# Attention behind a group norm: ten instead of four value units rounded in two parts, one batch's statistics moved to another engine, and another order at the end

## The reference, cut to what matters

```
h = group_norm(x, 8 groups over channels and positions) * gn_w + gn_b
q = qw h + qb;  k = kw h + kb;  v = vw h + vb            # 1x1 convolutions, C = 128
attn = softmax(q^T k / sqrt(128), over the 1024 keys)    # (4, 1024, 1024)
out  = x + pw (attn v) + pb
```

## Time and profile before

| | us |
|---|---|
| median of three runs | 138.47 |
| the profiled execution, its own time | 138.43 |
| its span | 136.2 |
| PE busy | 127.9 (94% of the span) |
| DVE busy | 101.1 (74%) |
| ACT busy | 70.0 (51%) |
| POOL busy | 40.4 (30%) |

### The profile page before, as it was taken

The page is one execution under the profiler, slowest core; times in us unless marked ns, Lnnn a source line. Parts: engine busy times, 40 slices in busy tenths (PEclk is TensorE's granted clock), DMA queues, the critical chain, the costliest instruction groups (busy, mean ns, idle before and its releaser), DMA issues.

```text
span 136.2 us, 2258 instructions
## 1 busy us (share of the span) xinstructions
PE 127.9 (94%) x759; PEld 111.6 (82%) x759; DVE 101.1 (74%) x172; ACT 70.0 (51%) x118; POOL 40.4 (30%) x39
## 2 busy tenths in 40 slices
PE   5899999949999999999999999999999999999990
PEld 5897878827768888999898898898988999988870
DVE  0577889999998878979689989856977898140222
ACT  4054687755765673547346977474585335331000
POOL 5053005085020251305026695024049220012000
PEclk9999999999999999999999999999999999999999
DMA  4970000001998599889961898899915998989512
GB/s 139 277 278 0 0 5 0 18 23 35 197 212 178 152 216 206 188 218 216 203 188 36 196 212 189 233 204 211 199 70 118 197 212 217 239 184 212 172 39 77
DMA packets 9566, 21.00 MB, mean 154 GB/s; under 512 B 2362, under 2 KB 4052, under 8 KB 9556
## 3 DMA queue, kind: packets, MB, share of 16 engines
q1 hardware_dynamic: 8816, 20.59, 62.1%
q10 hardware_dynamic: 740, 0.28, 0.8%
HBM read 4.07 MB, written 2.11 MB: 45 GB/s over the span
## 4 chain that ended last, share of the span: by engine, by line
PE 65%; SPq 12%; DVE 9%; issue 6%; DMA 5%; DVEq 0%
PE ACC L417 24%; SPq L205 11%; PE S L336 8%; PE S L337 7%; PE S L340 7%; PE A L316 5%; DVE blocks L735 3%; PE S L375 3%; DMA pT<-blocks 2%; DMA x_sb<-x 2%; DVE s_sb L726 2%; PE S L280 2%; PE A L292 1%; DVE bn L651 1%; PE A L293 1%
## 5 line engine op out<-in xcount | busy, mean ns | idle before, releaser
L726 DVE TENSOR_SCALAR_CACHE_REDUCE s_sb<-S,row_term 128x1024 f32<-128x1024 f32 x32 | 40.9, 1279 | 12.1 <-PE S L340 11.9
L417 PE MATMUL ACC<-pT,v 128*128 128x128 f32 (+1 forms) x288 | 45.8, 310 | 0.2 <-DMA pT<-blocks 0.2
L546 ACT ACTIVATE s_sb<-s_sb,rowmin 128x1024 f32<-128x1024 f32 x32 | 36.8, 1151 | 15.5 <-DVE s_sb L726 14.5
L417 PEld LDWEIGHTS ACC<-pT,v 128*128 128x128 f32 x288 | 40.3, 191 | 3.4 <-issue 0.6
L735 DVE STREAM_TRANSPOSE blocks<-s_sb 128x1024 f32<-128x1024 f32 x28 | 34.7, 1239 | 0.0
L336 PE MATMUL S<-h_hi,g_hi 128*128 128x512 f32 x64 | 28.7, 449 | 0.3 <-issue 0.3
L337 PE MATMUL S<-h_lo,g_hi 128*128 128x512 f32 x64 | 25.1, 393 | 0.0
L340 PE MATMUL S<-h_hi,g_lo 128*128 128x512 f32 x64 | 19.9, 392 | 0.0
L887 POOL TENSOR_TENSOR xb<-rden_bc,xb 128x512 f32<-128x512 f32 (+1 forms) x7 | 8.4, 1197 | 24.6 <-DVE rden_bc L755 18.9
L340 PEld LDWEIGHTS S<-h_hi,g_lo 128*128 128x128 f32 x64 | 12.0, 188 | 2.8
L336 PEld LDWEIGHTS S<-h_hi,g_hi 128*128 128x128 f32 x64 | 12.1, 189 | 2.3 <-issue 0.4
(11 more groups left out here) (100 smaller groups left out, 145.7 us busy)
## 6 DMA issues: line engine op xcount, KB each, us to landing
pT<-blocks SPq DMA_DIRECT2D x112, 128.0 KB, 2.5
rden_bc<-row_store SPq DMA_DIRECT2D x6, 256.0 KB, 3.5
x_sb<-x SPq DMA_DIRECT2D x1, 1024.0 KB, 6.6
out<-xb SPq DMA_DIRECT2D x8, 128.0 KB, 2.7
out<-xb SPq DMA_DIRECT2D x4, 256.0 KB, 3.1
x_sb<-x SPq DMA_DIRECT2D x2, 256.0 KB, 3.0
x_sb<-x SPq DMA_DIRECT2D x1, 512.0 KB, 3.9
w_in<-weights ACTq DMA_DIRECT2D x2, 128.0 KB, 3.5
```

The lines of the kernel that those rows point to most:

```text
L417: last = pe.matmul(to, v[:, b % 3, t, :], probs[:, :, t, :], start=(t == 0), stop=(t == KT - 1))
L546: act.activation(s_sb[:, c % 3, :], s_sb[:, c % 3, :], ACT.Exp, bias=rowmin[:, c % CH:c % CH + 1], scale=-1.0, accum_out=den[:, n % 2, k:k ...
L726: dve.tensor_scalar(s_sb[:, c % 3, :], S[:, c % 2, :], row_term[:, b % 2, i:i + 1], None, ALU.add, ALU.min, accum_out=rowmin[:, i:i + 1]). ...
```

## The change

- The split units are now (1,2), (1,3) and all four of sets 3 and 5: ten for four. Quarter u of sets 3 and 5 is rounded in step `FIRST[n] + 7 + u` (17 to 20, and 25 to 28), and its unit is computed in the next step. Set 1's two quarters are rounded at the end of step 10. v is rounded in steps 9, 15 and 23.
- Batch 2's statistics go from DVE to ACT: one pass with a sum (Identity) in step 6, one pass with a sum of squares (Square) in step 7, both writing a full result that nobody reads to the first 1024 columns of `pT`, and three small multiplications. PE takes them in step 8 instead of 7. SP's `move_set(2)` waits for them.
- Batch 1's group statistics go through PE one step earlier (steps 0 and 1), its shift stands ahead of the drain in step 3, and ACT normalises it in steps 3 and 4 instead of 4 and 5. The reciprocals of set 1 are turned in step 10 instead of 9.
- On DVE the row terms stand right behind the drain, ahead of the block transposes.
- At the end chunks 30 and 31 are two products of 128 columns each. Chunk 30's stands where the pair stood, chunk 31's at the very end; each is finished and stored by itself.

```diff
-TURN_STEPS = (3, 9, 11, 15, 19, 23, 27)
+TURN_STEPS = (3, 10, 11, 15, 19, 23, 27)
-DEVIATION_STEPS = (1, 7, 16)
-VARIANCE_STEPS = (2, 8, 17)
-EARLY_STATS_STEPS = (5, 6)
-SPLIT_SETS = (3, 5)
+DEVIATION_STEPS = (0, 8, 16)
+VARIANCE_STEPS = (1, 9, 17)
+CHANNEL_STEPS = (6, 7)
+SPLIT_UNITS = ((1, 2), (1, 3), (3, 0), (3, 1), (3, 2), (3, 3), (5, 0), (5, 1), (5, 2), (5, 3))
+SPLIT_SETS = (1, 3, 5)
+ROUND_V_STEPS = (9, 15, 23)
+    FIRST_QUARTERS = {FIRST[n] + 7: SPLIT_UNITS.index((n, 0)) for n in (3, 5)}
+    SECOND_QUARTERS = {FIRST[n] + 7 + u: SPLIT_UNITS.index((n, u)) for n in (3, 5) for u in (1, 2, 3)}
...
+            def last_chunk_unit(d):
...
+                for t in range(KT):
+                    last = pe.matmul(chunk_sums[d], v[:, L % 3, t, :], pair_T[:, t, d, :], start=(t == 0), stop=(t == KT - 1))
                 last.then_inc(part_done, 1)
...
             value_unit(DIRECT)
-            value_unit(DIRECT + 1)
             value_unit(FIRST[LS - 1] + 2)
             value_unit(FIRST[LS - 1] + 3)
+            value_unit(DIRECT + 1)
...
+            def channel_means():
...
+                act.activation(pT[:, 0, 0:N], x_sb[:, 2, :], ACT.Identity, accum_out=chan_sums[:, 0:1]).then_inc(sums_ready, 1)
+                act.wait_ge(sums_ready, 1)
+                act.mul(chan_sums[:, 1:2], chan_sums[:, 0:1], -1.0 / N).then_inc(sums_ready, 1)
+                act.mul(chan[:, 0:1], chan_sums[:, 0:1], 1.0 / N).then_inc(sums_ready, 1)
+            def channel_squares():
+                act.wait_ge(sums_ready, 3)
+                act.activation(pT[:, 0, 0:N], x_sb[:, 2, :], ACT.Square, bias=chan_sums[:, 1:2], accum_out=chan_sums[:, 2:3])\
+                   .then_inc(sums_ready, 1)
+                act.wait_ge(sums_ready, 4)
+                act.mul(chan[:, 1:2], chan_sums[:, 2:3], 1.0 / N).then_inc(chan_ready, 1)
...
+            def round_probs(r):
+                n, u = SPLIT_UNITS[r]
+                for a in (2 * (u // 2), 2 * (u // 2) + 1):
+                    act.wait_ge(moved[n % 2][a], MOVED * ((n + 1) // 2))
+                if r > 1:
+                    act.wait_ge(part_done, unit_end(r - 2))
+                    act.wait_ge(p_lo_ready, r - 1)
+                probs, hi, lo = split_views(r)
+                act.copy(hi, probs).then_inc(p_hi_ready, 1)
...
             # ACT, step c
+                if c in FIRST_QUARTERS:
+                    round_probs(FIRST_QUARTERS[c])
...
-                if late == 3 and b < L:
+                if i == 3 and b < L:
                     normalize_hi(b + 1, 0, HALVES)
-                if late == 4 and b < L:
+                if i == 4 and b < L:
                     normalize(b + 1)
...
-                        round_probs(n, c - FIRST[n] - 8)
+                if c in SECOND_QUARTERS:
+                    round_probs(SECOND_QUARTERS[c])
                 exponentials(c)
+                if c == CHANNEL_STEPS[0]:
+                    channel_means()
+                if c == CHANNEL_STEPS[1]:
+                    channel_squares()
+                if c in ROUND_V_STEPS:
+                    round_v(ROUND_V_STEPS.index(c))
+                if c == FIRST[1] + LAG:
+                    round_probs(0)
+                    round_probs(1)
...
             # POOL, step c
+                if c - 1 in ROUND_V_STEPS:
+                    split_v(ROUND_V_STEPS.index(c - 1))
+                if c in FIRST_QUARTERS:
+                    split_probs(FIRST_QUARTERS[c])
+                if c in SECOND_QUARTERS:
+                    split_probs(SECOND_QUARTERS[c])
+                if c == FIRST[1] + LAG:
+                    split_probs(0)
+                    split_probs(1)
                 if i == 4 and b < L:
                     split_h(b + 1)
                 if divided_in(c) is not None:
                     add_residual(divided_in(c))
```

More of the change, by code:

```diff
@@ L152, in build @@
         A1 = psum("A1", [P, BANK])
-        sums = [ACC[:, n % 2, 0:P * SETS[n]] for n in range(LS)] + [S[:, 1, 0:PN]]
+        sums = [ACC[:, n % 2, 0:P * SETS[n]] for n in range(LS)]
+        chunk_sums = [S[:, 1, BANK * d:BANK * d + P] for d in range(2)]
         last_sums = [ACC[:, (LS - 1) % 2, 0:UW], ACC[:, LS % 2, 0:UW]]
@@ L242, in _ @@
             store_set(LS - 2)
-            store_set(LS)
+            store_chunk(0)
             store_set(LS - 1)
-            sp.wait_ge(stored, 16 * (NS + sum(crosses(n) for n in range(NS))))
+            store_chunk(1)
+            sp.wait_ge(stored, 16 * (NS + 1 + sum(crosses(n) for n in range(NS))))
         @block.tensor
@@ L367, in first_set_part @@
                     last.then_inc(part_done, 1)
[L369 to L376, removed]
-                last.then_inc(part_done, 1)
@@ L387, in split_unit @@
                     t = PT * half + w
-                    pe.matmul(to, v_hi[:, t, :], p_hi[:, half, w, :], start=(t == 0), stop=False)
-                    pe.matmul(to, v_hi[:, t, :], p_lo[:, half, w, :], start=False, stop=False)
-                    last = pe.matmul(to, v_lo[:, t, :], p_hi[:, half, w, :], start=False, stop=(t == KT - 1))
+                    pe.matmul(to, v_hi[:, t, :], p_hi[:, r % 2, w, :], start=(t == 0), stop=False)
+                    pe.matmul(to, v_hi[:, t, :], p_lo[:, r % 2, w, :], start=False, stop=False)
@@ L391, in split_unit @@
+                    last = pe.matmul(to, v_lo[:, t, :], p_hi[:, r % 2, w, :], start=False, stop=(t == KT - 1))
                 last.then_inc(part_done, 1)
             def moved_unit(n, u):
-                if n in SPLIT_SETS and u > 1:
-                    split_unit(n, u - 2)
+                if (n, u) in SPLIT_UNITS:
+                    split_unit(n, u)
                     return
@@ L820, in _ @@
                 drain_scores(c)
-                if c == VARIANCE_STEPS[0] + 1:
-                    shift(1)
+                if late == 0:
+                    row_terms(b, 1)
+                if late == 2:
+                    row_terms(b, 2)
+                if i == 7 and b < L:
+                    row_terms(b + 1, 0)
                 if c - 2 in range(SETS[0]):
```

107 lines of the change are left out of this document (58 added, 49 removed).

## The result

The changed kernel takes 141.01 us (median of four runs), the kernel before, run beside it, 138.74. Its time is 1.018 times that of before, 95% interval 1.014 to 1.022. Run again later in other company it was 1.023 times (1.018 to 1.028). The comparisons leave out runs that a disturbance made much longer, of either kernel.

A forecast was written before the change was run, and what follows sets the result against it. PE, busy 127.9 of 136.2 us, was taken as the bound, with its waits for late inputs. From 138.43 us: -1.0 - 0.6 + 3.4 + 1.3 - 0.3 = +2.8, giving 141.2 us, range 138.4 to 142.8.

The forecast's parts named there:

- Set 3: Steps 18 to 21: PE waits for POOL's `p_lo` in three steps, +3.4 us, between +0.9 and +4.4.
- `h_lo` hidden by 0.9 us: After step 21's last `p_lo`: batch 3's `h_lo` ready at 86.0, wanted by PE at 86.9, so no wait.
- Set 5: Steps 26 to 29: PE waits 1.15 and 0.8 us for `p_lo`, +1.3 us, between +0.5 and +2.0.
- Set 1: Quarters rounded at the end of step 10, used in 12 and 13, covered by PE's work: -0.6 us, or 0.
- The early part: Steps 3 to 8: the 1.95 us wait for `h_lo` goes, statistics then wait 1.0: -1.0 us, between 0 and -1.95.
- The end: Last two products: PE +0.1, DVE -0.25, smaller last store -0.2; sum -0.3 us.
- The quarters come in time: Rival, POOL in steps 18 to 20: no waits, full gain, 135.2 us; chance 0.14 for in time or nearly.
- No gain early: Rival, early steps: freed 1.95 us go to statistics' wait and DVE, 142.2 us; slower rivals together 0.12.
- set 1's roundings: Rival, steps 10 and 11: ACT's rounding delays batch 2's `h`, +0.5 to +1 us; slower rivals together 0.12.
- Square reloading tables: Rival, ACT in step 7: two table loads around the Square pass, +1.3 to +2.6 us, 142.5 to 143.8; chance 0.04.

The follow-up runs named there:

- the two experiments: Changed kernel with ACT's roundings of steps 19 and 20 ahead of `h_hi` and `h`: 139.05 us; changed kernel with batch 3's shift ahead of step 18's drain: 139.55 us.

## Why the prediction was right, step by step

- **Set 3, +3.4 forecast, +3.7 measured.** The waits were put at 1.15, 1.98 and 0.95. Counted in the same way, from the unit before plus 2.80, they are 1.21, 1.94 and 1.15 (the records' idle times are 1.07, 1.70 and 0.92). The last remainder ended 0.13 later than put and PE began 0.14 behind it instead of 0.07, and the last unit took 1.51 instead of 1.43; that is the 0.3. The method did the work: the instructions that would be late stood in the trace of before, and only the consumer was moved against them.
- **What held them**, of the same step: I named ACT's order and DVE's held shift, and the two experiments give 2.0 and 1.9 us back, of which they share some 1.1. But I took "PE waits for the remainder" for the whole cost. With the remainder unread, 3 of 5 us stay, mainly in late roundings and in `h_lo`. I had `h_lo` hidden by 0.9 us; that holds only as long as PE waits.
- **Set 5, +1.3 and +1.4**, with waits of 1.15 and 0.8 forecast and, counted in the same way, 1.21 and 0.80 measured (1.07 and 0.54 idle).
- **Set 1, -0.6** in the account; leaving it out cost 0.8 of span, and another 0.5 outside the span, which I had not foreseen.
- **The early part, -1.0 forecast, -0.5 measured.** The chain came as written: `h_lo` in time, then 0.90 for `g_lo`, then the statistics. Counted from the start of scores 0, PE began the value tiles and the statistics' product each 0.2 later than put, and step 10 took back some 0.25 by a second wait for `g_lo`: PE's value tiles begin 0.72 us behind its last scores product there, 0.47 before. This term was mis-sized, toward the optimistic side.
- **The end, -0.3 forecast, -1.0 in the trace after.** DVE's 0.26 and the store's 0.4 (2.0 from issue to the end of the span instead of 2.4) were in the sum, the store at half its size. The other 0.4 is a wait for set 7's first transfers that the trace of before had and I left out of the sum; PE comes 4.2 us later now and the transfers 3.6, so it vanishes. It is no merit of the new order, which by itself gave nothing that could be told.
- **The rivals.** "The quarters come in time" was ruled out by the five waits. "No gain early" fell with the 0.5 us of the early part, and set 1's roundings were free. For Square reloading tables the trace speaks plainly: there is one table load, and the Square pass took 1.14 us (the early stretch above). The Trainium skill's page ScalarE: Activation LUTs, section "Table sets: the hidden batching unit", would price a switch at about 2.7 us; no switch happened here between exp, Identity and Square.
- **The total.** Two terms erred by 0.5 and 0.7 us in opposite directions, and set 3 by 0.3. The span grew by 3.2 us where the sum had 2.8, and the 0.5 us outside the span, which no term had, brought the execution to +2.7. So the waits of sets 3 and 5 were foreseen, and that 141.2 stands so close to 141.01 is luck.

## What to carry to other kernels

When a producer keeps its place and its consumer is moved a step ahead, subtract in the trace you have: the producer's end less the consumer's new start is the wait, before anything is built. Then look at what stands behind the late producer in its queue, because that wait hides further ones. And before putting work on an idle engine, look at the steps in which it is idle: POOL was busy 30% of the time, but in steps 18 to 21 of the changed kernel it was busy for 8.4 of 11.1 us, and the rest it waited for ACT. An idle engine also needs its input in time: the order of the instructions ahead of it cost more there than its own time.

## What the runs showed of the hardware

**A tiny DVE instruction is held by a long one of POOL.** The shift works on 128 numbers. It took 0.18 to 0.22 us where POOL stood still. In step 19 it took 1.68 to 1.72 where POOL's 2.4 us instruction was running, and ended with it (eleven traces, among them). Two experiments take POOL's instruction away from beside it. With POOL's remainders left out, the same instruction in the same place is

```profile
72.43 0.18 DVE L741 SCALAR_TENSOR_TENSOR gshift<-neg_mean,gscale,cols 128x1 f32<-128x1 f32 x1
```

and moved to step 18 it took 0.22. When it comes later in POOL's instruction it is held for less: 0.67 us at 43.57 in the changed kernel, where POOL's `v_lo` still had 0.65 to run, and 0.89 in the earlier trace rows. The drains and block transposes beside the same POOL instructions kept their 1.28 and 1.24. The Trainium skill's page SBUF — State Buffer, section "SBUF: two separate sides", calls the port pair that DVE and GpSimd share an exclusive lock, held for the whole instruction by whichever starts first, and names among the DVE instructions that need it those with two inputs in SBUF, against a GpSimd instruction that reads SBUF. The shift has its inputs in SBUF and POOL's subtraction reads there, so by that rule the shift should wait for POOL's end, and the traces agree; the drain, which reads its scores from PSUM, and the transpose, with one input, don't have two such inputs, and they were not held.

**PE's clock at half behind a wait of about 2 us, in some runs.** The kernel before has one of 1.95 us in step 6. Of its 58 runs made beside the experiments, 17 had a mean clock of 0.983 to 0.988 and took 140.1 us or more, the other 41 took 137.9 to 139.5. So it was in the two experiments that keep such a wait: 5 of 12 runs with only the end changed, and 7 of 12 with the statistics back on DVE. The trace of the kernel with only the end changed is one of these (the half clock is only part of its 143.32 us): PE idle for 1.94 until 34.16, then, in the columns of the stretches above,

```profile
33.00:36.00 3.00, 1.84 (x4) 1.49 (x5) 3.00 (x5) 1.46 (x4) 3.00 (x3) 0.70 0.00 0
36.00:39.00 3.00, 3.00 (x14) 2.50 (x13) 1.47 (x5) 0.80 (x2) 0.31 (x1) 0.73 0.50 108
39.00:42.00 3.00, 2.53 (x16) 1.97 (x16) 3.00 (x7) 1.68 (x3) 0.00 (x0) 1.00 0.92 199
```

Of the 66 runs of kernels in which that wait is split into two of at most 1.03 us, none had a mean clock under 0.998, though the ten of the changed kernel wait 1.7 us in step 20. So the early part is worth more over many runs than its 0.5 us: with it, the 2 us that three runs in ten lost are gone. That it is the wait and nothing else about these kernels is argued from the counts, and why the same wait comes with the lower clock in some runs and not in others is not settled here.
